# Last stage of a two-layer kernel: eight loads on GpSimd's queue, batch 0 ahead in products, norm and router, and a shorter rank of the router's entries

## The reference

```python
h = _layernorm(x) * (1 + ca) + sa
x = x + ga * attention(h)            # 128 heads of width 4, then out @ Wo
h = _layernorm(x) * (1 + cb) + sb
# FFN
base_out = h @ base_W.T + base_b
probs = softmax(h @ router_W.T + router_b)      # 15 entries
topk_p, topk_i = top_k(probs, 8)
w = weights of the 8 experts (entries mapped by expert_map)
lora = (h @ A * w) @ B * 2.0                    # 8 experts of rank 16
x = x + gb * (base_out + lora)
```

## Time and profile before

| what | us |
|---|---|
| three timed runs | 2174.14, 2176.51, 2177.23 |
| their median | 2176.51 |
| the profiled execution: own time | 2175.61 |
| its span in the trace | 2173.8 |

### The profile page before, as it was taken

The page is one execution under the profiler, slowest core; times in us unless marked ns, Lnnn a source line. Parts: engine busy times, 40 slices in busy tenths (PEclk is TensorE's granted clock), DMA queues, the critical chain, the costliest instruction groups (busy, mean ns, idle before and its releaser), DMA issues.

```text
span 2173.8 us, 42824 instructions
## 1 busy us (share of the span) xinstructions
PE 2122.4 (98%) x11276; PEld 1644.1 (76%) x11276; DVE 1732.3 (80%) x3095; ACT 1341.9 (62%) x2709; POOL 1357.7 (62%) x1621
## 2 busy tenths in 40 slices
PE   7999999999999999999999999999999999999978
PEld 4788888888886757777777777777777777777756
DVE  6787788788777758888888888888888877788764
ACT  2443443433433568888888888888888865555532
POOL 4766766766753447777777777777777721365334
PEclk9999999999999999999999999999999999999999
DMA  7010010010004153222222222222222222444441
GB/s 249 26 43 30 20 48 29 19 48 29 19 20 121 37 189 108 71 73 78 74 78 65 77 78 74 76 66 79 75 77 69 75 79 76 138 130 124 114 130 40
DMA packets 138991, 165.82 MB, mean 76 GB/s; under 512 B 30261, under 2 KB 72917, under 8 KB 138916
## 3 DMA queue, kind: packets, MB, share of 16 engines
q1 hardware_dynamic: 135076, 152.31, 24.5%
q0 software_dynamic: 3840, 12.59, 2.0%
HBM read 101.52 MB, written 29.10 MB: 60 GB/s over the span
## 4 chain that ended last, share of the span: by engine, by line
PE 87%; DVE 7%; issue 2%; ACT 1%; POOL 1%; SPq 1%; DMA 1%; DVEq 0%; ACTq 0%; POOLq 0%
PE bank L2593 12%; PE bank L2578 11%; PE bank L2600 11%; PE bank L2155 7%; PE bank L2157 7%; PE bank L2156 7%; PE bank L2510 6%; PE bank L2508 5%; PE bank L2509 5%; PE bank L2623 3%; PE bank L2633 3%; PE bank L2628 2%; DVE rope_b L1631 1%; DVE rope_a L1630 1%; DVE rope_b L1632 1%
## 5 line engine op out<-in xcount | busy, mean ns | idle before, releaser
L1934 DVE TENSOR_REDUCE mcol<-bank 128x1 fp32r<-128x512 f32 x1024 | 684.1, 687 | 186.8 <-PE bank L2578 176.7
L2593 PE MATMUL bank<-q,k 128*128 128x512 f32 x1024 | 417.9, 408 | 0.0
L2578 PE MATMUL bank<-km,q 128*128 128x512 f32 x1024 | 406.0, 397 | 3.5 <-ACT q L1374 2.5
L2600 PE MATMUL bank<-q,k 128*128 128x512 f32 x1024 | 404.0, 395 | 0.0
L2578 PEld LDWEIGHTS bank<-km,q 128*128 128x128 f32 x1024 | 317.6, 310 | 53.0 <-DVE mcol L1934 3.9
L1413 ACT ACTIVATE pT<-bank 128x512 f32<-128x512 f32 x416 | 228.1, 602 | 113.7 <-PE bank L2600 111.9
L1413 ACT ACTIVATE x<-bank 128x512 f32<-128x512 f32 x416 | 227.7, 601 | 88.7 <-PE bank L2600 86.5
L2593 PEld LDWEIGHTS bank<-q,k 128*128 128x128 f32 x1024 | 192.3, 188 | 84.7 <-issue 27.9
L2600 PEld LDWEIGHTS bank<-q,k 128*128 128x128 f32 x1024 | 192.9, 188 | 31.7
L2510 PE MATMUL bank<-hT_hi,wr_lo 128*128 128x512 f32 x512 | 205.5, 401 | 0.0
L2508 PE MATMUL bank<-hT_hi,wr_hi 128*128 128x512 f32 x512 | 202.3, 395 | 0.1
(11 more groups left out here) (372 smaller groups left out, 5061.5 us busy)
## 6 DMA issues: line engine op xcount, KB each, us to landing
q<-q SPq DMA_DIRECT2D x256, 128.0 KB, 2.3
wst<-in_L_attn_Wq_rope SPq DMA_DIRECT2D x64, 256.0 KB, 3.1
o_d<-ost SPq DMA_DIRECT2D x63, 256.0 KB, 3.1
st_q<-in_L_attn_wq SPq DMA_DIRECT2D x8, 1024.0 KB, 7.6
st_wo<-in_L_attn_wo SPq DMA_DIRECT2D x8, 1024.0 KB, 5.4
q<-qc_d SPq DMA_DIRECT2D x256, 32.0 KB
km<-kc_d SPq DMA_DIRECT2D x256, 32.0 KB
k<-kc_d SPq DMA_DIRECT2D x256, 32.0 KB
```

Source lines behind the costliest of these rows:

```text
L1934: dve.tensor_reduce(mcol[:, k % 2, i % 4, i // 4:i // 4 + 1], bank[4 + i % 2][:], AX.X, ALU.max, negate=True)\
L2578: pe.matmul(bank[4 + i % 2][:], q2[:, k % 4, h, i % 4:S:4], km[:, b, h], start=True, stop=True).then_inc(max_mm, 1)
L2593: pe.matmul(bank[s % 4][:], k1[:, k % 2, t], q1[:, k % 4, h], start=True, stop=False)
L2600: pe.matmul(bank[s % 4][:], k2[:, k % 2, h, t], q2[:, k % 4, h], start=False, stop=True).then_inc(scores1, 1)
```

## The change

- **Loads.** The eight loads of `load_last_sums` leave SP's queue for GpSimd's, behind the low part of Wo's first two quarters and ahead of the last two. `last_den` and `last_add` wait for all eight.
- **Order.** TensorE does all products of batch 0, then those of batch 1, with the transposes of batch 0's norm between `first_heads` and `last_heads` of batch 1; `router(0)` comes before the transposes of batch 1, `low_rank_in(0)` before `router(1)`. VectorE, ScalarE and GpSimd follow that order. The norm of batch 0 is written to the two halves of `hT_lo` (high and low part), that of batch 1 to the halves of `hT_hi`, so batch 0 needn't wait for Wo's last use. `xn2` and `full2` lie elsewhere for that.
- **Rank.** A difference and one comparison with a margin (0 or the smallest normal float) take the place of two comparisons, a product and a sum.
- **Low rank.** ScalarE copies `h @ A` out of its bank, and one VectorE operation multiplies the bank of the spread weights by 2.0 and by that copy; the copy of the spread weights (`kept_spread`, twice) is gone.

```diff
@@ memory
+        with ExitStack() as normed_rows:
+            xn2 = sbuf_in(normed_rows)("xn2", [P, NT, D])
@@ where the norm is written and read
+        def normed(ph, b):
+            if ph == 3:
+                h = (hT_lo, hT_hi)[b]
+                return h[:, :, 0:S], h[:, :, S:2 * S]
+            return hT_hi[:, :, b * S:(b + 1) * S], hT_lo[:, :, b * S:(b + 1) * S]
...
-        OUT_TILES = (0, 3, 5, 6, 1, 2, 4, 7)
+        OUT_TILES = (0, 3, 2, 6, 1, 5, 4, 7)
@@ SP
             for u in range(LOOP, UNITS + 1):
-                if u == UNITS - 1:
-                    load_last_sums(0)
-                    load_last_sums(1)
                 period(u, u % 4)
@@ GpSimd
             wo1_low((0, 1))
+            load_last_sums(0)
+            load_last_sums(1)
             wo1_low((2, 3))
@@ ScalarE
+            def low_rank_copy(b):
+                act.wait_ge(r_hmm, b + 1)
+                act.activation(lri[:, b * S:(b + 1) * S], bank[4 * b + 1][:], ACT.Copy).then_inc(r_copied, 1)
...
             norm_std(3, 0)
+            norm(3, 0, (0,))
+            norm(3, 0, (1,))
+            norm(3, 0, (2,))
+            norm(3, 0, (3,))
             weights_high1(KT)
             weights_high1(KT + 1)
-            norm(3, 0, (0,))
-            norm(3, 0, (1,))
             norm_std(3, 1)
-            norm(3, 0, (2,))
-            norm(3, 0, (3,))
+            router_parts(0)
             norm(3, 1, (4,))
@@ VectorE, rank
-                dve.tensor_tensor(cmpg[:], p_m, p_n, ALU.is_gt)
-                chain(dve.tensor_tensor(cmpe[:], p_m, p_n, ALU.is_equal))
-                chain(dve.tensor_tensor(cmpe[:], cmpe[:], before[:].unsqueeze(1).broadcast_to([P, NT, NR, NR]), ALU.mult))
-                chain(dve.tensor_tensor(cmpg[:].rearrange("p t n m -> p (t n m)"), cmpg[:].rearrange("p t n m -> p (t n m)"),
-                                        cmpe[:].rearrange("p t n m -> p (t n m)"), ALU.add))
+                chain(dve.tensor_tensor(cmpe[:], p_m, p_n, ALU.subtract))
+                chain(dve.tensor_tensor(cmpg[:], cmpe[:], margin[:].unsqueeze(1).broadcast_to([P, NT, NR, NR]), ALU.is_ge))
                 chain(dve.tensor_reduce(rank[:].rearrange("p t n -> p (t n)"), cmpg[:].rearrange("p t n m -> p (t n) m"), AX.X, ALU.add))
@@ TensorE, behind the transposes of the base weights
+            for t in range(TB):
+                first_heads(t)
+            for t in range(TB):
+                last_heads(t)
+            for t in range(TB, NT):
+                first_heads(t)
+            norm(3, 0)
+            for t in range(TB, NT):
+                last_heads(t)
             turn_low_rank(KT)
             turn_low_rank(KT + 1)
             turn_low_rank(KT + 2)
+            router(0)
+            norm(3, 1)
+            low_rank_in(0)
             base(1)
-            router(0)
             router(1)
             router_sums()
-            low_rank_in(0)
+            base(2)
             base(0)
             low_rank_in(1)
-            base(2)
+            base(4)
             base(3)
+            base(5)
             turn_kept(0)
             turn_kept(1)
             spread_kept(0)
             spread_kept(1)
             base(6)
-            base(4)
             low_rank_out(0)
             low_rank_out(1)
             low_rank_out(2)
-            base(5)
             low_rank_out(3)
             low_rank_out(4)
+            base(7)
             low_rank_out(5)
             low_rank_out(6)
-            base(7)
             low_rank_out(7)
```

More of the change, by code:

```diff
@@ L303, in adaln_two_layers @@
         ehot = sbh("ehot", [16, P])
-        before = sbh("before", [P, NR, NR])
+        margin = sbh("margin", [P, NR, NR])
+        sbh("m_pad", [P, 2408])
+        full2 = sbh("full2", [P, 4, S])
         g1.close()
@@ L659, in _ @@
                     period(4 * g + k, k)
-            def load_last_sums(b):
-                stored = range((H1 - 32) // 2, DIRECT // 2)
-                for i in range(2):
-                    sp.wait_ge(o_stored[i], 16 * len(range(i, DIRECT // 2, 2)))
-                sp.wait_ge(oo_split, EARLY - 1 + b)
-                for par in range(2):
-                    for dst, r in zip(SUMS[b], (0, DEN)):
-                        sp.dma_start(dst[0:2 * HD1 * len(stored), par], sums_of(stored, par, b, r)).then_inc(sums_loaded[b], 16)
             def load_wo1(ks):
@@ L706, in _ @@
             sp.dma_start(ecol[:], a["expert_of_column"]).then_inc(g_loaded, 16)
[L707 to L708 removed]
+            sp.dma_start(margin[:].rearrange("p n m -> p (n m)"),
+                         a["entry_margin"].rearrange("n m -> (n m)").rearrange("(o k) -> o k", o=1).partition_broadcast(P)
                          .rearrange("p o n -> p (o n)")).then_inc(g_loaded, 16)
@@ L1017, in _, with load_last_sums @@
                     sums_times(n)
+            def load_last_sums(b):
+                stored = range((H1 - 32) // 2, DIRECT // 2)
+                for i in range(2):
+                    pool.wait_ge(o_stored[i], 16 * len(range(i, DIRECT // 2, 2)))
+                pool.wait_ge(oo_split, EARLY - 1 + b)
+                for par in range(2):
+                    for dst, r in zip(SUMS[b], (0, DEN)):
+                        pool.dma_start(dst[0:2 * HD1 * len(stored), par], sums_of(stored, par, b, r)).then_inc(parts_loaded, 16)
             wo1_low((0, 1))
+            load_last_sums(0)
+            load_last_sums(1)
             wo1_low((2, 3))
             def last_add(b):
-                pool.wait_ge(sums_loaded[b], 64 + 128)
+                pool.wait_ge(parts_loaded, 128 * EARLY + 128)
+                pool.wait_ge(sums_loaded[b], 128)
                 o = SUMS[b][0]
@@ L2755, in router @@
                 at = slice(b * S, (b + 1) * S)
-                for i, h in enumerate((hT_hi, hT_lo)):
+                for i, h in enumerate(normed(3, b)):
                     for k in range(KT):
-                        e = pe.matmul(bank[4 * b][32 * k:32 * k + 32, :], rwT[:, k], h[:, k, at].bitcast(F32), start=(i == 0), stop=(i == 1))
+                        e = pe.matmul(bank[4 * b][32 * k:32 * k + 32, :], rwT[:, k], h[:, k].bitcast(F32), start=(i == 0), stop=(i == 1))
                 e.then_inc(r_part, 1)
@@ L2773, in low_rank_in @@
                 at = slice(b * S, (b + 1) * S)
-                mm3(bank[1 + b][:], [(laT_hi[:, k], laT_lo[:, k], hT_hi[:, k, at], hT_lo[:, k, at]) for k in range(KT)], r_hmm)
+                hi, lo = normed(3, b)
+                mm3(bank[4 * b + 1][:], [(laT_hi[:, k], laT_lo[:, k], hi[:, k], lo[:, k]) for k in range(KT)], r_hmm)
             def base(i):
                 t = OUT_TILES[i]
-                at = slice(t * P, (t + 1) * P)
-                if t == 0:
-                    pe.wait_ge(r_copied, 1)
-                elif t in (1, 2):
-                    pe.wait_ge(r_hfull, t)
-                elif t == 4:
-                    pe.wait_ge(r_wexp, 1)
-                elif t == 7:
-                    pe.wait_ge(r_wexp, 2)
+                hi, lo = normed(3, t // TB)
+                at = slice(t % TB * P, t % TB * P + P)
+                if t in (0, 1, 5):
+                    pe.wait_ge(r_copied, {0: 1, 1: 2, 5: 4}[t])
+                elif t in (4, 7):
+                    pe.wait_ge(r_hfull, {4: 1, 7: 2}[t])
                 else:
                     wait_norm(pe, 3, t // TB)
-                if i == 0:
-                    pe.wait_ge(g_lo, KT)
                 for k in range(KT):
-                    pe.matmul(bank[t][:], hT_hi[:, k, at], bwT_hi[:, k], start=(k == 0), stop=False)
-                    pe.matmul(bank[t][:], hT_hi[:, k, at], bwT_lo[:, k], start=False, stop=False)
-                    pe.matmul(bank[t][:], hT_lo[:, k, at], bwT_hi[:, k], start=False, stop=False)
+                    pe.matmul(bank[t][:], hi[:, k, at], bwT_hi[:, k], start=(k == 0), stop=False)
+                    pe.matmul(bank[t][:], hi[:, k, at], bwT_lo[:, k], start=False, stop=False)
+                    pe.matmul(bank[t][:], lo[:, k, at], bwT_hi[:, k], start=False, stop=False)
             def low_rank_out(i):
@@ L2902, in shape_constants @@
         "expert_of_column": np.broadcast_to(np.arange(P) // R1, (16, P)).astype(np.float32),
-        "entry_before": (n[None, :] < n[:, None]).astype(np.float32),
+        "entry_margin": np.where(n[None, :] < n[:, None], 0.0, np.finfo(np.float32).tiny).astype(np.float32),
     }
```

103 lines of the change are left out of this document (38 added, 65 removed).

## The result

The changed kernel takes 2181.02 us (median of 11 runs, 2177.61 to 2185.48), the kernel before beside it 2175.43 (11 runs, 2173.32 to 2178.59): ratio 1.0027, 95% interval 1.0018 to 1.0036. It is slower by 5.6 us; the forecast was 1 us faster. The profiled execution took 2180.82 us, its span is 2179.0.

What follows compares the result with a forecast made beforehand. The end was bound by when VectorE begins the last sums, its chain to batch 1's rows and TensorE's remaining work; -2.9 + 3.0 + 0.5 - 2.9 + 1.2 = -1.1 us against 2175.61 gave 2174.5, range 2170.5 to 2177.5.

Steps and rivals of the forecast that it cites:

- term A: Loads ahead of VectorE's last denominators: batch 0's last sums land at 2084.0 in place of 2086.88, -2.9 us.
- Rival 4: Loads on GpSimd's queue land late, each us behind 2084.0 costing one; chance 0.10, and 0.05 for beyond 0.2%.
- term B: VectorE's chain from the first denominators to the rows of batch 1 grows to 35.5 us, +3.0 us.
- the packed stretch: DMA engines busy for 0.96 of 2071 to 2084; its end, 2084.0, was taken as the sums' landing.
- The wait for tile 4: VectorE, done with batch 0's rows, waits for TensorE's tile 4 of the products, +1.5 us.
- collisions of VectorE and GpSimd: The two engines exclude each other in VectorE's chain: +2.5 against -2.3, that is +0.2 us.
- C: From the rows of batch 1 to the second router: router(0) stands before the transposes at a low clock, +0.5 us.
- rival 1: TensorE's clock stays at 2.4 GHz through the shorter wait before batch 1's rows: -2.0 there, total 2172.0; chance 0.22.
- D: TensorE's work from the second router to its end: low_rank_in(0) leaves it, 12 matmuls, -2.9 us.
- E: From TensorE's end to the last addition: GpSimd's seven additions end later, then VectorE's last one, +1.2 us.
- The rank at nothing: Two rank operations fewer, of 2.03 us, save nothing, as the kept weights are ready before TensorE asks.

Runs made afterwards that it cites:

- e10: Changed kernel with one more GpSimd load of the same form, its data unused, some 20 us ahead of the eight; ratio 1.0011.
- e11: Changed kernel with one unused GpSimd load ahead and last_heads(4) to (7) ahead of the transposes of batch 0's norm; ratio 1.0005.
- e12: Kernel before with the eight loads on GpSimd's queue and one unused GpSimd load ahead of them; 2173.88 us, ratio 0.9986.
- e15: Kernel before with eight loads on GpSimd, one unused load ahead, the rank in three operations and low_rank_in(0) ahead of base(1); 2169.86 us, ratio 0.9975.
- e13: Kernel before with only the rank changed, to three operations; ratio 1.0001.
- e14: Kernel before with only low_rank_in(0) moved from behind the second router to ahead of base(1); 2179.37 us, ratio 1.0018.
- e16: Kernel before, loads on SP, with the rank in three operations and low_rank_in(0) ahead of base(1); 2173.16 us, ratio 0.9988.
- e1_loads_back: Changed kernel with the eight large loads back in SP's queue; 2179.97 us, ratio 1.0013.
- e5: Changed kernel with GpSimd's first load issued as two loads of half the partitions each; one run, 2183.91 us.
- e6: Changed kernel with SP's loads of Wo's last two quarters and the 1 MB base weights held back until GpSimd's eight have landed; one run, 2189.74 us.
- e2: Kernel before with only the eight loads moved to GpSimd's queue; 2177.34 us, ratio 1.0005.
- e7: Changed kernel with the low part of Wo's last two quarters between GpSimd's first load and the other seven; ratio 1.0022.

## Why the prediction was wrong

The step that failed is term A, "the loads: -2.9 us". Rival 4, loads that land late, is what happened: the denominators start at 2090.45, or 2089.2 without the 1.26 us, next to the 2089.5 that the prediction named as the point of slower by over 0.2%. That case had a chance of 0.05, on the argument that a GpSimd load lands in 6.6 us at most. The first load landed within that, in 6.5 us; what failed is the issue of the other seven, which waited for it.

Step by step the ratios add up like this: the loads without the pause make the old order 3.0 us faster (0.9986), the new order with its other parts costs 5.4 (1.0011), the pause another 3.5 (1.0027). The forecast had -2.9 for the loads with their issue, and they measure +1.1 alone (1.0005); it had +1.8 for all the rest, which measures +4.8 on top of them. The two misses are 4.0 and 3.0 us; the first is term A, the second lies mostly in term B.

- **A, loads (-2.9, measured +2.3).** Two errors. The larger: GpSimd's loads were costed at 0.58 us each from rows with 24 loads, none of which met the pause. Nor were these spaced out: with 24 loads of `vc` between them, GpSimd issued eight in a row from 1843.18 to 1848.5 without a gap. The cost was right for the first 48 loads and wrong at the 49th. The pause moved the denominators by 2.4 us in the profiles (14.12 with it, 11.73 without) and held up Wo's low part, with TensorE's 4.67 us and a low clock; both together are worth 3.5 us at the end (1.0027 against 1.0011), and 4.1 in the old order (1.0005 against 0.9986). The smaller: without the pause the denominators hardly come earlier. Four profiles with these loads (e10, e11, e12, e15) have them at 11.73, 11.47, 13.76 and 10.87 us behind the copy. Four of the old order with SP's loads (before, e13, e14, e16) have 11.81, 13.53, 11.67 and 11.78, and I had 8.9. I put the landing at the end of the packed stretch. In e10_one_before the DMA engines are 1.02 busy until 2084, 0.77 to 2086 and 0.16 to 2088, and the last small load, issued within 0.5 us of where I had it, lands at 2088.0: 6.5 us behind its issue. The prediction had 1.88 for that by itself and 3.4 with the packed stretch (2080.6 to 2084.0).
- **B, VectorE's chain (+3.0, measured +3.8).** Right in kind, too small in size. The wait for tile 4 is 1.45 us where I had 1.5. But the term counts -2.3 us for collisions of VectorE and GpSimd that the new order avoids, and the old order avoids most of them too when the denominators come at another moment (e12, e13, e15). And the earlier sums that were to pay for the longer chain did not come. Against the old order with the same loads the chain is 4.4 us longer with the pause (36.29 and 31.89) and 6.4 without (36.04 in e11 and 29.64 in e12). The measured price of the whole order is 2.8 us with SP's loads (e1_loads_back, 1.0013), 4.8 with the pause (1.0027 against 1.0005) and 5.4 without (1.0011 against 0.9986). The tile 4 part of it is 1.3 to 1.5 us.
- **C (+0.5, measured -1.6).** The clock fell as forecast, so rival 1 did not come; yet most of its gain did. `router(0)` took 3.47 us, nearly all at half clock (forecast 3.3), and the 16 transposes behind it 1.97 us, not the 3.65 of the earlier trace rows: the clock rose just before them (0.73 over 2127 to 2128, 1.00 over 2128 to 2129), 3 us into the work, where before it stayed low to 2126.6, 6 us into it. Rival 1 cites the Trainium skill, page "TensorE: Matmul & The Clock Gate", section "What's actually happening", for the rule that activity releases the throttle; the trace agrees: `router(0)` was that activity, and I had counted only its length. The size is not firm. In the other profiles of the new order this piece is 10.49 to 11.71 us, the last in e10_one_before.
- **D (-2.9, measured -1.2).** The mechanism holds: in e10_one_before it is 35.16 us to TensorE's last matmul, forecast 35.1. In the profiled execution of the changed kernel the clock was 0.52 for 3.5 us of it, which is the 1.6 us that are missing. In the old order the early low-rank product gains only together with the short rank (e14, e16).
- **E (+1.2, measured +1.0).** Right: seven additions without a pause.
- **The rank at nothing.** Right, alone (1.0001) and in the change: the kept weights are ready at 2150.57 and TensorE asks at 2157.62, 7 us later, as forecast. That it is the condition for term D in another order was not seen.

The rule of the Trainium skill, page "SBUF — State Buffer", section "SBUF: two separate sides", that GpSimd's loads wait while VectorE holds the ports, doesn't explain the pause: VectorE works 0.00 us of 2074 to 2080. The Trainium skill, page "DMA: Bandwidth & Descriptors", section "Terms", says that GpSimd writes its descriptors (the records that tell a DMA engine what to move) to rings in SBUF. A full ring fits e5, e6 and e10, but no run here shows one.

What stays open: that the fixed place is a full memory of descriptors is argued, not shown. Shown is that it stands behind the same bytes of GpSimd's loads (e5), that it moves with one load more (e10), and that it ends 0.9 us behind the landing of GpSimd's own load. The 1.6 us that are left in e10, with no load under way, are not explained. The gain of the loads without the pause is timed (0.9986), but where it arises is seen only in part.

## What to carry to other kernels

Try a queue that is moved to another engine by itself, before an order is built on it: 48 loads at 0.55 to 0.75 us each said nothing of what the 49th would hold up, and one edit (e2) showed it. Where such a pause ends with a landing, one load that goes out earlier and lands in time takes most of it away (e10). Before reordering for one batch, look which engine bounds the piece up to that batch's result: here it was VectorE, and TensorE's order could gain nothing there. A collision that the kernel before shows isn't a cost of its order until a second execution shows it too. An edit that costs nothing because something else hides it should be tried together with the one that takes that cover away.

## What was not expected of the hardware

- The issue of GpSimd's loads stood still for 3.6 to 8.4 us at one fixed place of its sequence, behind its 49th load, until 0.9 us behind that load's landing. Only further loads were held up, not its arithmetic (e7).
- From the third to the eighth, GpSimd's issues grow from 0.58 to 0.71 us.
- TensorE's granted clock fell to 0.50 while it was fully busy, in some executions: 0.52 over 2161.5 to 2165 in the changed kernel (3.50 us busy), 0.66 over 2155 to 2160 in e12_old_order (5.00 us busy). Both times it fell some 4 us behind the start of the transposes of the kept weights, which 0.33 us of waiting follow; before and in e10_one_before it stayed at 1.00 behind the same work. An estimate from these shares is 1.7 us lost each time. It may be a part of the spread between runs; only the profiled executions show it.
